# VectorE: side work of a row pair ahead of the first block's eviction in a seven-product period

## The reference

```python
h = jnp.maximum(_layernorm(x, axis=-1), 0.0)
lQ, lK, lV = masked_x @ Wlq, h @ Wlk, h @ Wlv + blv
gQ, gK, gV = masked_x @ Wgq, h_bar @ Wgk, h_bar @ Wgv + bgv      # h_bar: mean row of h
es, eV = masked_x @ Wes, masked_x @ Wev + bev
local = where(adj, lQ @ lK.T * scale, -1e9);  glob = gQ @ gK.T * scale
m = max(max(local, axis=1), glob, es)
le, ge, ee = exp(local - m), exp(glob - m), exp(es - m)
denom = sum(le) + ge + ee
out = x + maximum(le / denom @ lV + ge / denom * gV + ee / denom * eV, masked_x)
```

## Time and profile before

| | before |
|---|---|
| median of 3 runs | 729.88 us |
| profiled execution | 730.02 us, span 728.2 us |
| PE busy | 722.5 us (99%), 5248 matmuls |
| DVE busy | 566.3 us (78%) |
| ACT busy | 532.3 us (73%) |
| POOL busy | 432.9 us (59%) |
| granted TensorE clock | 0.999 of full speed, mean |
| 0 to 143.3 us (two products a block) | PE busy 141.63 us |
| 143.3 to 687 us (seven-product stage) | PE busy 542.79 of 543.70 us |
| 687 to 728.2 us (the end) | PE busy 38.06 of 41.20 us |

### The profile page before, as it was taken

The page is one execution under the profiler, slowest core; times in us unless marked ns, Lnnn a source line. Parts: engine busy times, 40 slices in busy tenths (PEclk is TensorE's granted clock), DMA queues, the critical chain, the costliest instruction groups (busy, mean ns, idle before and its releaser), DMA issues.

```text
span 728.2 us, 15018 instructions
## 1 busy us (share of the span) xinstructions
PE 722.5 (99%) x5248; PEld 512.6 (70%) x5248; DVE 566.3 (78%) x1347; ACT 532.3 (73%) x709; POOL 432.9 (59%) x300
## 2 busy tenths in 40 slices
PE   9999999999999999999999999999999999999998
PEld 7667566667666777776767676676777776676787
DVE  6975988777877788878887887878878787877645
ACT  6884967858677776776878687678767777777690
POOL 4779889455565465556545655566556545644584
PEclk9999999999999999999999999999999999999999
DMA  9784877879779888988978797989888798887796
GB/s 301 131 175 84 158 152 155 155 139 211 158 159 178 166 163 146 214 151 175 170 166 161 157 201 137 195 158 179 171 170 161 150 206 150 178 170 179 135 183 152
DMA packets 364620, 121.93 MB, mean 167 GB/s; under 512 B 324736, under 2 KB 364544, under 8 KB 364544
## 3 DMA queue, kind: packets, MB, share of 16 engines
q1 hardware_dynamic: 364000, 120.44, 82.0%
q10 hardware_dynamic: 544, 0.52, 0.2%
HBM read 36.57 MB, written 4.19 MB: 56 GB/s over the span
## 4 chain that ended last, share of the span: by engine, by line
PE 87%; issue 4%; POOL 3%; DVE 3%; ACT 1%; DMA 1%; DVEq 0%; POOLq 0%; ACTq 0%
PE ps_u L1126 13%; PE ps_u L1128 13%; PE ps_u L1130 13%; PE ps_x L1025 7%; PE ps_x L1024 7%; PE ps_x L1023 7%; PE ps_q L947 4%; PE ps_v L1023 3%; PE ps_v L1025 3%; PE ps_v L1024 3%; POOL p_base L621 2%; PE ps_w L1023 2%; PE ps_w L1025 2%; PE ps_w L1024 2%; PE ps_q L1192 1%
## 5 line engine op out<-in xcount | busy, mean ns | idle before, releaser
L621 POOL TENSOR_TENSOR p_base<-s,p_base 128x1024 f16<-128x1024 f32 x112 | 241.8, 2159 | 228.9 <-ACT p_base L824 228.6
L1126 PE MATMUL ps_u<-v_rows,pT_base 128*128 128x256 f16 x944 | 257.3, 273 | 0.0
L1130 PE MATMUL ps_u<-v_rows,pT_base 128*128 128x256 f16 x944 | 257.3, 273 | 0.0
L1128 PE MATMUL ps_u<-v_rows,pT_base 128*128 128x256 f16 x944 | 257.3, 273 | 0.0
L787 ACT ACTIVATE bias<-adj,big 128x1024 f32<-128x1024 uint8 x127 | 156.5, 1236 | 130.7 <-DVE bmax L1495 128.5
L800 ACT ACTIVATE s<-s,negm,invc 128x1024 f32<-128x1024 f32 x128 | 157.0, 1226 | 8.9 <-DVE negm L1551 8.9
L824 ACT ACTIVATE p_base<-s 128x1024 f16<-128x1024 f32 x122 | 128.9, 1057 | 4.8 <-POOL p_base L621 1.0
L1128 PEld LDWEIGHTS ps_u<-v_rows,pT_base 128*128 128x128 f16 x944 | 92.4, 98 | 52.0
L1126 PEld LDWEIGHTS ps_u<-v_rows,pT_base 128*128 128x128 f16 x944 | 92.4, 98 | 52.0
L1495 DVE CUSTOM_DVE_ANT_0 s<-ps_x,bias 128x512 f32<-128x512 f32 x128 | 87.2, 686 | 48.2 <-PE ps_x L1025 44.7
L1130 PEld LDWEIGHTS ps_u<-v_rows,pT_base 128*128 128x128 f16 x944 | 92.4, 98 | 10.6
(11 more groups left out here) (242 smaller groups left out, 1292.2 us busy)
## 6 DMA issues: line engine op xcount, KB each, us to landing
adj<-adj SPq DMA_DIRECT2D x64, 256.0 KB, 3.2
pT_base<-p_base SPq DMA_TRANSPOSE x234, 3.2
s<-x SPq DMA_DIRECT2D x7, 512.0 KB, 7.7
f32q<-mx SPq DMA_DIRECT2D x14, 256.0 KB, 3.6
xm<-x SPq DMA_DIRECT2D x14, 256.0 KB, 3.1
xm<-mx SPq DMA_DIRECT2D x14, 256.0 KB, 3.5
out<-t_sb SPq DMA_DIRECT2D x14, 256.0 KB, 2.6
mxT_f<-mxT SPq DMA_DIRECT2D x4, 256.0 KB, 3.1
```

The lines of the kernel that those rows point to most:

```text
L621: nc.gpsimd.tensor_tensor(p_rows(u)[:, 1], s32[:, p % NS, u % 2], p_rows(u)[:, 0], ALU.subtract).then_inc(s_plo, 1)
L1126: nc.tensor.matmul(acc, turn[:, 0, j], v_rows[:, kc, 0:D], start=opens, stop=False, skip_group_check=True)
L1128: nc.tensor.matmul(acc, turn[:, 0, j], v_rows[:, kc, D:2 * D], start=False, stop=False, skip_group_check=True)
L1130: done = nc.tensor.matmul(acc, turn[:, 1, j], v_rows[:, kc, 0:D], start=False, stop=end, skip_group_check=True)
```

## The change

In a seven-product period, `out11(p)` moves from ahead of `q_row_scales`, the second `side_rows`, `row_max` and `weights` to behind them. It stays behind `es_rows` and ahead of `local_rows`. Nothing is added or removed, and every instruction keeps its waits. In step 0 `row_max` passes `out11`, in step 1 `q_row_scales` and `weights`, in step 2 `side_rows(done, 1)`.

```diff
@@ -1829,8 +1829,6 @@
                         mx_scale((p + 5) // NG)
                     if step == 3 and ended:
                         es_rows(done)
-                    if p < NPER:
-                        out11(p)
                     if project:
                         q_row_scales(m)
                     if step == 2 and ended:
@@ -1839,6 +1837,8 @@
                         row_max(n)
                     if step == 1 and ended:
                         weights(done)
+                    if p < NPER:
+                        out11(p)
                     if step == 3 and ended:
                         local_rows(done)
```

## The result

The changed kernel takes 732.06 us (median of seven runs, 731.49 to 732.42) against 729.88 (729.72 to 730.03): 2.18 us more, a ratio of 1.0029 with a 95% interval of 1.0019 to 1.0039. Its profiled execution took 732.35 us with a span of 730.5. The forecast was 728.8, in a range of 728.5 to 731.0, with 0.15 for a slowdown of over 0.2%. The kernel became slower where it was to become faster, and the time lies outside the range.

The account below looks back on a forecast made before the run. TensorE's set amount of matmul work was taken as the limit, busy 99% of the span. Removing the 1.07 us hole with 0 added gave 729.88 - 1.07 = 728.8 us, range 728.5 to 731.0.

Parts of the forecast that it names:

- The hole before `p5(19)`: TensorE's wait behind `out12(18)`, after side rows that waited for GpSimd; the new order closes it, minus 1.07 us.
- The shift of step 1: Scales and weights ahead of `out11` make `out12` and then period 38's first `p_low` later by 0.47 to 1.5 us.
- The double wait of the row maximum: In step 0 the row maximum ahead of `out11` can wait twice for GpSimd, adding up to 1.0 us of shift.
- the order in step 2: Period 38: second side row goes in behind the running `p_low`, then `q_low`; `out12` ends earlier, 0.9 us to spare.
- case D: The hole of period 18 comes back somewhere in the first three pairs, margin 0.05 at `p5(18)`: 729.9 us; chance 0.12.
- What is late next is `q_low`, which has over 15 us until its pair starts: Period 18 after the change: GpSimd's `q_low` ends at 217.21, later than 217.03, with over 15 us of room.
- no queue of SP is passed: VectorE issues no DMA, so only the inputs of the exponentials and masks were said to come earlier.
- nothing changes in step 3: Step 3 keeps its order: `es_rows` was already ahead of `out11` and `local_rows` stays behind.
- signs of being wrong: Wrong as a whole if TensorE shows holes at `p6`, `p7` or `p2`, read as having 1 us and more of margin.
- B: Steady pairs, step 2: `q_low` gets the port before the side row, 0.32 us a pair, 732.3 to 734.1; chance 0.15.
- C: Tight spots at `p5` cost 0.1 us in five pairs or up to 0.2 in eleven: 729.3, at most 731.0; chance 0.16.

Follow-up runs that it names:

- the load first: The whole change, plus SyncE issuing the load of the next masked rows ahead of the transpose of the queries: 729.12 us, 0.9987 against the kernel before.
- two of the three parts: Two kernels, both with the load ahead of the transpose: steps 1 and 2 changed, 730.35 us; steps 0 and 2 changed, 730.48 us.

## Why the prediction was wrong

**What held.** The path: TensorE's work is the limit and all that changed is holes. The hole before `p5(19)` closed by the steps given: side rows issued at 213.76 (forecast 213.87), the second ended at 217.47 (217.49), `out12` ended at 218.69 (218.7). The shift of step 1: in the changed kernel the first `p_low` of period 38 starts 5.9 us after the period's start instead of 4.4, a shift of 1.5, the upper end of 0.47 to 1.5. The double wait of the row maximum (0.94 and 2.09 us in period 36), and with it the order in step 2: the side row waits for `p_low`, goes in behind it, `q_low` follows, and `out12` of period 38 ends 0.78 us before `p5(39)` (forecast: 0.9 to spare). With the load first, the sum nearly came out: 729.12 against 728.8, with two holes of 0.24 and 0.18 us in between, the first at `p5(18)`, where case D had a margin of 0.05, the second behind the first side rows of period 62.

**What failed.** One sentence, with the one that it leans on: "What is late next is `q_low`, which has over 15 us until its pair starts", and "no queue of SP is passed". I followed `q_low` to its last user, the next pair's `p1`, and not to what is queued behind its first user on SyncE. `transpose_q` isn't urgent; `load_mx`, behind it, had 0.3 us of cover. So I let `q_low` slip by 1.5 us at a price of nothing, and it cost 18.4 us of waiting for the rows in ten pairs (1.0 us in three before), of which TensorE saw 0.27 to 0.65 us in five, 2.49 us together. A second sentence failed with it: "nothing changes in step 3". The order there is the old one, but `mx_scale` now met both `p_low` of that step, at 1.3 to 2.0 us each. The "over 15 us" was misread too: in the earlier trace rows and the stretches of the earlier trace rows `q_low` ends at 217.03 and the pair starts at 229.15, 12.1 us later; that alone would have cost nothing. None of the signs of being wrong named `p1`, where the holes then stood.

**The rivals.** B (side rows lose the port) wasn't what made the changed kernel slow: its side rows win. It is real with two of the three parts, for 0.30 to 0.36 us a pair against the 0.32 worked out, but in five pairs, not eleven. C's 0.10 us in five pairs is what the side rows alone show. That the measured 732.06 lies near B's 732.3 is chance: another mechanism made it. Neither rival names the load, so the time fell outside the range though their prices per pair were near what the runs show.

**The rule weighed against the rows.** The Trainium skill (SBUF — State Buffer, Who interferes with whom) has it, of the VectorE modes that use two ports, that whoever issues first has the shared pair for its whole instruction and the other fully blocks. Of a VectorE instruction with two SBUF inputs, which a side row is, it says only that it contends with a GpSimd instruction that reads SBUF. In the reading that a GpSimd instruction counts as issued once its input is there, the side row would lose to `q_low` in every pair. The changed kernel decides against that reading. ScalarE, VectorE and GpSimd in period 38:

```profile
423.55 0.93 ACT L764 ACTIVATE q_hl<-f32q 128x896 f16<-128x896 f32 x1
```

```profile
424.80 1.34 DVE L1591 SCALAR_TENSOR_TENSOR r_base<-gv_b,w,blv_b 128x256 f32<-128x256 f32 x1
```

```profile
423.72 2.14 POOL L621 TENSOR_TENSOR p_base<-s,p_base 128x1024 f16<-128x1024 f32 x1 [3.07 <-ACT p_base L824]
425.81 2.06 POOL L606 TENSOR_TENSOR q_hl<-f32q,q_hl 128x896 f16<-128x896 f32 x1
```

The input of `q_low` was there at 424.48, the side row came at 424.80, and yet it ended at 426.14, 0.28 us after the `p_low`, with `q_low` behind it (2.06 us instead of the 1.89 of the earlier trace rows). It loses when it comes after the end of the `p_low`, as at 339.58.

All 14 traces bear this out. They have 163 places where the first instruction of a side row (L1591) meets two of GpSimd's that follow each other without a gap. In 135 of them VectorE's instruction before the row ended 0.11 us or more before GpSimd's first: the row always went in between (it ended 0.27 to 0.30 us after that one, and GpSimd's next took 0.18 us longer). In 28 it ended 0.02 to 0.08 us after: the row always waited for GpSimd's next. Nine of these 28 are in the kernel before, among them the row at 425.53 of the earlier trace rows. So what counts here is whether the row is issued before GpSimd's current instruction ends, which is what rival B was weighed by.

**What stays open.** Why late and less late pairs alternate, in the kernel before too (margins of 0.33 and 0.22), wasn't tried. Nor is it shown by a run of its own by which way steps 0 and 1 together come to 5.5 us: their profile has the holes behind the side rows, but not why so many.

## What to carry to other kernels

When a producer gets later, follow each of its users, and on an in-order queue also everything behind that user: the cover of a chain is the smallest one among them, not that of the result it was made for. Before moving side work, list the instructions that wait for a DMA ahead of something that TensorE needs, with the time between landing and use; put the load with 0.3 us of cover ahead of the transfer with 7 us of it (the transpose of 301.54 lands 4.0 us later, and the pair starts at 312.56), and only then fill the gaps. Parts of a reordering that collide with another engine don't add up (0.55 and 0.55 made 5.5 us, and the third part took back 3.4), so the parts must be run together as well as alone.

## What I had not expected of the hardware

An instruction on 128x2 or 128x4 elements that takes 0.17 us alone takes 1.43, 1.99 or 2.14 us when it comes into a `p_low` of GpSimd, so the price of small side work is set by GpSimd's timetable and not by its own size. Who gets the port next is decided within 0.13 us around the end of GpSimd's instruction: a side row ready 0.11 us before it goes in next (0.48 us in all), one ready 0.02 us after it pays 2.18 us.
